# Output products put off by one step, and the first splits given to ScalarE and VectorE, in a four-stage attention and expert kernel

## The chip, the cores and the metric

One core of a Trainium2 chip runs the whole program. The metric is device time in microseconds (us), from the start to the end of one execution. Below, PE is TensorE's matmul side, PEld its weight loads, DVE is VectorE, ACT is ScalarE, POOL is GpSimd and SP is SyncE, whose queue issues the DMAs.

## What is computed

2048 tokens of width 512 go through two layers. All four parts are residual additions on `x`:

```python
x = x + L0_xattn(layernorm(x), ctx)   # 32 heads of 128, 8 key/value groups, biases
x = x + L0_ffn(layernorm(x))          # relu(x@up)**2 @ down, a latent branch, layernorm
x = x + L1_xattn(layernorm(x), ctx)   # 32 heads of 16
x = x + L1_ffn(layernorm(x))          # 8 experts, the two with the largest gate logits
```

The change is inside the first part:

```python
q = (query @ Wq + bq).reshape(B, L, NKV, G, HDIM)
k_, v_ = jnp.split(kv @ Wkv + bkv, 2, axis=-1)
attn = jax.nn.softmax(einsum('bkglm', q, k) * scale)
o = einsum('blkgd', attn, v).reshape(B, L, NHEAD * HDIM)
return o @ Wo + bo
```

## The kernel before

Every fp32 operand is split into two fp16 halves, high and low ("hi" and "lo"), and a product is three passes of fp16 matmuls (`group3`, L624): hi by hi, hi by lo, lo by hi. A product with an inner dimension of 512 is therefore 12 matmuls of 128x512. hi is written by ACT (or POOL), lo is the source less hi, written by DVE (or POOL).

The first attention runs in 32 steps `s`. A step takes one chunk of 512 tokens (8 batches of 64) for one group of four heads; the four chunks come first, then the next group. Steps 0 to 3 and 28 to 31 are written out, steps 4 to 27 are a loop of three rounds with eight steps each. Every engine has its own `b_step` with its order written by hand, and semaphores join them. On PE one step is, in this order:

- `b_scores`: 48 matmuls of 128x64 into banks 2 and 3;
- `proj(0..2)`: three of the four query projections of the **next** step (`b_proj`), into banks 0 and 1 in turn;
- `b_turn`: 16 transposes of the probabilities (L661), which need the low halves of the probabilities, `plo` on DVE (L1449, signal `s_plo`);
- `proj(3)`, `b_pv` 0 and 1 (L675, banks 6 and 7), `proj(4)` (keys), `b_pv` 2 and 3, `proj(5)` (values);
- `b_out` 0 to 3: the output products of this step, banks 4 and 5, added into `X` on DVE by `add` (L1463, signal `y_add`).

DVE's part of a step: `shift` (maximum and subtraction, L1431 and L1433, two halves), `prob` (sum, reciprocal, scaling, L1440 to L1444, two halves), `plo`, and between them the low halves of the projections (L1378; `proj(5)` is L1390), of the attention outputs (`olo`, L1378 too) and the four `add`. ACT's part: the two exponentials (L1059), `phi` (L1063), the high halves of the projections (L1024 to L1032), the copies of the turned probabilities (L1067) and of the outputs (L1038).

A projection into a bank must wait until the low half two projections back has been taken from it (`p_lo`). So `proj(2)` waits for the low half of `proj(0)`, and `proj(3)` for that of `proj(1)`.

Steps 0 and 1 have extra work: the layer norm of chunks 2 and 3 (`stats` L515 to L523, Newton steps L491 to L497, `xnorm` L535, `xlo` L542, eight transposes per tile, L554). The contexts of chunks 1 to 3 and the output weights of group 0 are split by POOL (`split_fine`, L370 to L378), the weights of group 1 by POOL as well (`group_piece`, L340 to L354), and POOL adds the output bias into `X` (`add_bo`, L399) between them. `proj(4)` of steps 0 to 2 waits for the context's low half. In the loop POOL starts on the weights of the next group when the outputs of the last one are done (`y_mm`), and on two further pieces of weights for later stages (`spare_piece`), five pieces in every four steps.

SP's queue loads in the order in which the code lists them; each load into one of the two slots of `raw` waits for the split of the piece before.

Of the kernel before, what the change touches and what calls it, by code (L numbers as in the profile page):

```python
# [67 lines left out]
def build(nc, x, ctxT, wB, wX, biasB, bo, gam, bet, lnw, be, bg, w_split, out):  # L68
    with ExitStack() as stack:
# [61 lines left out]
        staged = AW[:, 6144:10240]  # L131

# [88 lines left out]
        def _(sp):  # L221
# [20 lines left out]
            piece(4, ctxT[1], 0)  # L242
# [85 lines left out]
        def _(pool):  # L328
# [34 lines left out]
            def split_fine(conv, src, hi, lo, scale):  # L363
                n = src.shape[1]
                cuts = [slice(a, a + FINE) for a in range(0, n, FINE)]
                if scale is None:
                    pool.sem_inc(w_scaled, 1)
                else:
                    for q in cuts:
                        last = g.tensor_scalar(src[:, q], src[:, q], scale, 1.0, ALU.mult, ALU.mult)  # L370
                    last.then_inc(w_scaled, 1)
                    pool.wait_ge(w_scaled, conv + 1)
                for q in cuts:
                    last = g.tensor_scalar(hi[:, q], src[:, q], 1.0, 1.0, ALU.mult, ALU.mult)
                last.then_inc(w_hi, 1)
                pool.wait_ge(w_hi, conv + 1)
                for q in cuts:
                    last = g.tensor_tensor(lo[:, q], src[:, q], hi[:, q], ALU.subtract)  # L378
                last.then_inc(w_lo, 1)

            def landed(k):
                pool.wait_ge(raw_in[k % 2], 16 * (k // 2 - 1))

            def ctx_piece(k, c):
                landed(k)
                chunk = CT[:, c].rearrange("p s k n -> p s (k n)")
                split_fine(k, raw[:, k % 2, :], chunk[:, 0], chunk[:, 1], None)

            def group_piece(k, slot, arrivals, par, j):
# [3 lines left out]
                split(k, raw[:, slot, 0:n], hi, lo)  # L393
# [16 lines left out]
            for counted in (w_scaled, w_hi, w_lo):  # L410
                pool.sem_inc(counted, 3)
# [26 lines left out]
            for j in range(3):  # L438
                group_piece(7 + j, (7 + j) % 2, (7 + j) // 2 - 1, 1, j)
            add_bo(2)  # L440
            add_bo(3)
# [170 lines left out]
        def _(pe):  # L612
# [17 lines left out]
            def b_proj(s, c, par, j, place=None):  # L630
# [3 lines left out]
                if isinstance(s, int) and 0 < s < NC and j == 4:  # L634

                    pe.wait_ge(w_lo, s + 4)
# [28 lines left out]
            def b_pv(s, jb):  # L665
# [3 lines left out]
                if jb >= 2:  # L669
                    pe.wait_ge(o_lo, s * 4 + jb - 1)  # L670
                out_v = banks[6 + jb % 2].rearrange("p (h b l) -> p h b l", h=HG, b=2)
# [40 lines left out]
            def b_step(s, c, par, last, norm=None, split=None):  # L712
# [9 lines left out]
                b_scores(s, 1)  # L722
# [1155 lines left out]
```

## Time and profile before

| | us |
|---|---|
| median of 3 runs | 1924.45 (1923.99 to 1928.38) |
| the profiled execution | 1919.03 |
| its span, first to last instruction | 1917.2 |
| PE busy in the span | 1791.1 (93%) |
| DVE busy | 1255.0 (65%) |
| ACT busy | 894.4 (47%) |
| POOL busy | 534.5 (28%) |

Most of the runs agree closely with one another; the profiled execution is 5.4 us below the median. The trace gives start and length of each merged run of instructions on an engine, the idle time before it, and the instruction that ended this idle time. A run of 12 matmuls is listed as 2.75 us, but the next run starts 2.59 us after it: the last end is modelled and overlaps.

### The profile page before, as it was taken

The page shows a single profiled execution, that of the slowest core. Times are in us where ns is not written, and L with a number is a line of the kernel's source. Part 1 is how long each engine was busy: PE and PEld are TensorE (multiplying, and loading weights), DVE is VectorE, ACT ScalarE, POOL GpSimd, SP SyncE. Part 2 cuts the span into 40 slices and gives each one's busy share as a digit, 9 for nine tenths or more (in the row PEclk, how much of TensorE's full clock was granted, in tenths as well). Part 3 has the DMA queues.
Part 4 walks back from the last instruction along what each step waited for, and adds up shares of the span by engine and source line. Part 5 has one row for each costly group of instructions (what it writes and reads, how often), then busy time and mean ns, then how long its engine had stood idle before and what let it go on. Part 6 is the DMA issues. An engine that isn't in the chain of part 4 may idle for free. (4 is left out here: it accounts for less than half of the span.)

```text
span 1917.2 us, 36220 instructions
## 1 busy us (share of the span) xinstructions
PE 1791.1 (93%) x14128; PEld 986.1 (51%) x14128; DVE 1255.0 (65%) x2284; ACT 894.4 (47%) x1429; POOL 534.5 (28%) x403
## 2 busy tenths in 40 slices
PE   5899999999999999999999999985999999999997
PEld 2545555554555555555555444443555555555553
DVE  6785656556565556565656677767677777777763
ACT  5453434343434333343434333325666666666662
POOL 2960803407016062084000000000223222322333
PEclk9899999999999999999999999996999999999999
DMA  5220301203104012034100300030000000000000
GB/s 214 77 79 1 124 21 45 100 1 111 34 1 143 1 68 78 1 127 170 57 1 19 142 1 1 0 126 7 7 7 6 13 6 7 7 12 6 7 12 12
DMA packets 18378, 88.82 MB, mean 46 GB/s; under 512 B 2608, under 2 KB 2864, under 8 KB 10160
## 3 DMA queue, kind: packets, MB, share of 16 engines
q1 hardware_dynamic: 18224, 86.58, 12.4%
q8 instruction: 120, 1.97, 0.4%
q14 instruction: 34, 0.28, 0.0%
HBM read 65.60 MB, written 20.97 MB: 45 GB/s over the span
## 5 line engine op out<-in xcount | busy, mean ns | idle before, releaser
L624 PE MATMUL bank<-R 128*128 128x512 f16 (+1 forms) x7152 | 1301.0, 341 | 17.2 <-DVE R L1378 3.6
L624 PEld LDWEIGHTS bank<-R 128*128 128x128 f16 x7152 | 585.0, 98 | 655.9 <-issue 22.0
L1378 DVE SCALAR_TENSOR_TENSOR R<-bank,biases,R 128x512 f16<-128x512 f32 x288 | 203.2, 744 | 141.0 <-ACT R L1024 99.7
L475 POOL TENSOR_TENSOR R<-R 128x512 f32<-128x512 f32 x112 | 157.1, 1403 | 450.4 <-ACT R L1218 449.2
L1059 ACT ACTIVATE AW<-AW 128x512 f32<-128x512 f32 x64 | 40.3, 630 | 320.5 <-DVE AW L1433 320.5
L1463 DVE SCALAR_TENSOR_TENSOR X<-bank,X 128x512 f32<-128x512 f32 x128 | 88.3, 691 | 133.4 <-PE bank L624 132.5
L340 POOL TENSOR_SCALAR R<-R 128x2048 f32<-128x2048 f32 (+1 forms) x21 | 35.6, 1697 | 454.0 <-PE bank L624 450.2
L1218 ACT ACTIVATE R<-R,msk 128x512 f32<-128x512 f32 x128 | 90.3, 716 | 57.4 <-DVE R L1693 57.4
L1024 ACT ACTIVATE R<-bank,biases 128x512 f16<-128x512 f32 x128 | 87.0, 683 | 61.3 <-PE bank L624 59.9
L1390 DVE SCALAR_TENSOR_TENSOR R<-bank,R 64x512 f16<-64x512 f32 x64 | 44.0, 688 | 101.1 <-ACT R L1032 100.7
L1693 DVE SCALAR_TENSOR_TENSOR R<-bank,R 128x512 f32<-128x512 f32 x128 | 86.9, 679 | 29.0 <-PE bank L624 28.2
L1032 ACT ACTIVATE R<-bank 64x512 f16<-64x512 f32 x128 | 75.7, 592 | 56.1 <-PE bank L624 55.0
L461 POOL MEMSET R<- 128x256 f16 x1 | 0.3, 317 | 362.6 <-PE bank L624 362.6
L624 PE MATMUL bank<-CT,R 128*128 128x512 f16 x384 | 89.4, 383 | 12.7 <-DVE CT L1352 11.7
L624 PE MATMUL bank<-R,CT 128*128 128x128 f16 x1536 | 92.8, 221 | 0.0
L624 PEld LDWEIGHTS bank<-R,CT 128*128 128x128 f16 x1536 | 90.3, 99 | 1.0
L624 PE MATMUL bank<-AW,R 128*128 128x512 f16 x384 | 89.6, 384 | 1.1 <-ACT R L561 1.1
L354 POOL TENSOR_TENSOR R<-R 128x512 f16<-128x512 f32 x70 | 89.4, 1306 | 1.8
L1038 ACT ACTIVATE R<-bank,biases 128x512 f16<-128x512 f32 x128 | 80.8, 685 | 1.7 <-PE bank L675 1.7
L354 POOL TENSOR_TENSOR AW<-R,AW 128x512 f16<-128x512 f32 x64 | 77.9, 1249 | 1.3
L561 ACT ACTIVATE R<-bank 128x1024 f16<-128x1024 f16 x64 | 64.4, 1017 | 27.9 <-PE bank L554 27.9
L675 PE MATMUL bank<-AW,R 128*128 128x256 f16 x512 | 67.5, 275 | 6.4 <-DVE R L1378 5.5
(145 smaller groups left out, 2101.8 us busy)
## 6 DMA issues: line engine op xcount, KB each, us to landing
R<-in_wB SPq DMA_DIRECT2D x16, 1024.0 KB, 5.8
R<-in_wX SPq DMA_DIRECT2D x16, 1024.0 KB, 4.9
w_split<-AW SPq DMA_DIRECT2D x16, 1024.0 KB, 4.8
R<-w_split SPq DMA_DIRECT2D x12, 1024.0 KB, 7.3
R<-in_wB SPq DMA_DIRECT2D x8, 512.0 KB, 5.5
R<-in_ctxT SPq DMA_DIRECT2D x4, 1024.0 KB, 10.0
X<-in_x SPq DMA_DIRECT2D x4, 1024.0 KB, 14.1
out<-X SPq DMA_DIRECT2D x16, 256.0 KB, 2.0
```

The source lines that it names most:

```text
L354: last = g.tensor_tensor(lo[:, q], src[:, q], hi[:, q], ALU.subtract)
L475: g.tensor_tensor(acc, acc, tmp[:, e % 2, :], ALU.add).then_inc(e_acc, 1)
L561: nc.scalar.activation(dst, banks16[bank][:, 0:2 * KC * P].rearrange("p (a n) -> p a n", a=2 * KC), ACT.Copy).then_inc(n_stored, 1)
L624: last = pe.matmul(dst, a(sa), b(sb_), start=(k == 0), stop=(k == m - 1))
L675: last = pe.matmul(out_v[:, :, bb, :], V[:, b, p, :], PTb[:, b * 256:(b + 1) * 256], start=(p == 0), stop=(p == 1))
L1024: sc.activation(qT[:, 0, :, j, :], banks[j % 2].rearrange("p (b l) -> p b l", l=64), ACT.Identity, bias=bias_col(g * HG, j)).then_inc(p_hi, 1)
L1032: last = sc.activation(V[64 * half:64 * half + 64, odd:BC:2, 0, :], v[64 * odd:64 * odd + 64], ACT.Copy, scale=UN)
L1038: sc.activation(oT[:, 0, :, jb * P:(jb + 1) * P], banks[6 + jb % 2].rearrange("p (h n) -> p h n", h=HG), ACT.Identity, bias=bias_col(g, 40 ...
L1218: sc.activation(dst, tmp[:, e % 2, :], ACT.Relu, scale=msk[:, 16 + e:17 + e]).then_inc(e_rel, 1)
L1378: v.scalar_tensor_tensor(out=dst, in0=src, scalar=bias, in1=hi, op0=ALU.add, op1=ALU.subtract).then_inc(done, 1)
L1463: v.scalar_tensor_tensor(out=xt, in0=banks[4 + t % 2], scalar=UN2, in1=xt, op0=ALU.mult, op1=ALU.add).then_inc(y_add, 1)
L1693: v.scalar_tensor_tensor(out=tmp[:, e % 2, :], in0=banks[2 + e % 2], scalar=UN, in1=beb[:, e, :], op0=ALU.mult, op1=ALU.add).then_inc(e_bi ...
```

## The change

- **Output products.** For steps 0 and 1 `b_out` stays at the end of the step (`early`). The products of step 2 and later are issued in the step after: two of them behind the scores, `proj(0)`, the other two, then `proj(1)` and `proj(2)`. They use banks 6 and 7 in place of 4 and 5, which they share with `b_pv`, and the first waits for `olo(2)`, the others for `olo(3)`; `b_pv` 0 and 1 of a step wait for the last two `add` of the step before.
- **DVE.** `add_last(0)` follows `prob(0)`, `add_last(1)` follows `prob(1)`; the low half of `proj(0)` moves from behind `prob(0)` to behind `plo(1)`, and the last two additions follow it.
- **First contexts and output weights.** The split of chunk `s+1`'s context is done inside steps 0 to 2: high half on ACT behind `phi(1)` and ahead of `proj(0)`, low half on DVE behind `proj(0)` and ahead of `stats` and `proj(1)`. `proj(1)` now follows `stats`. The output weights of group 0 are split before step 0 (ACT behind the high half of the first query projection, DVE at the very end).
- **POOL.** It starts, once the projections for step 0 are done, with the key and value weights of group 1 (loaded into a place of their own, `raw_kv1`), then the query weights and the output weights, and adds the output bias chunk by chunk after the outputs of group 0 of that chunk have been added.
- **SP.** The order of the loads and their waits follow.

The diff, cut:

```diff
             x_chunk(1)
-            piece(4, ctxT[1], 0)
+            sp.dma_start(raw[:, 0, :], ctxT[1]).then_inc(raw_in[0], 16)
...
+            sp.dma_start(raw_kv1, wB[1, :, 2048:3072]).then_inc(raw_in[0], 16)
             sp.wait_ge(ctx_lo, 1)
-            piece(5, ctxT[2], 0)
-            piece(6, ctxT[3], 5)
-            for j, (a, b) in enumerate(cuts):
-                piece(7 + j, wB[1, :, a:b], 6 + j)
+            sp.dma_start(raw[:, 1, :], ctxT[2]).then_inc(raw_in[1], 16)
+            sp.wait_ge(ctx_lo, 2)
+            sp.wait_ge(ctx_hi, 2)
+            sp.dma_start(raw[:, 0, :], ctxT[3]).then_inc(raw_in[0], 16)
+            sp.wait_ge(ctx_lo, 3)
+            sp.dma_start(raw[:, 1, :], wB[1, :, 0:2048]).then_inc(raw_in[1], 16)
+            piece(9, wB[1, :, 3072:5120], 9)
...
             def add_bo(c):
+                pool.wait_ge(y_add, (c + 1) * TC)
                 for t in range(c * TC, (c + 1) * TC):
-                    pool.wait_ge(n_xn, t + 1)
...
-            pool.wait_ge(p_lo, 4)
-            pool.wait_ge(o0_in, 16)
-            split_fine(3, raw_o0, *halves(R2, 6144, 2048), WS)
-            ctx_piece(4, 1)
-            pool.wait_ge(const_in, 48)
-            add_bo(0)
-            ctx_piece(5, 2)
-            ctx_piece(6, 3)
-            add_bo(1)
...
+            pool.wait_ge(p_lo, 6)
+            group_piece(7, 0, 2, 1, 1, raw_kv1)
+            group_piece(8, 1, 2, 1, 0)
+            group_piece(9, 1, 3, 1, 2)
+            pool.wait_ge(const_in, 48)
+            for c in range(NC):
+                add_bo(c)
...
             def b_out(s, par, t):
-                pe.wait_ge(o_lo, s * 4 + t + 1)
+                pe.wait_ge(o_lo, s * 4 + (3 if t == 0 else 4))
...
-                group3(banks[4 + t % 2], [(lambda p, h=h: oT[:, p, h, t * P:(t + 1) * P],
+                group3(banks[6 + t % 2], [(lambda p, h=h: oT[:, p, h, t * P:(t + 1) * P],
...
-                for j in range(3):
-                    proj(j)
+                out(0)
+                out(1)
+                proj(0)
+                out(2)
+                out(3)
+                proj(1)
+                proj(2)
...
                 exp(0)
                 exp(1)
-                proj(0)
                 phi(0)
                 phi(1)
+                if isinstance(s, int) and s < NC - 1:
+                    act.wait_ge(raw_in[s % 2], (32, 16, 48)[s])
+                    sc.activation(CT[:, s + 1, 0].rearrange("p k n -> p (k n)"), raw[:, s % 2, :], ACT.Copy).then_inc(ctx_hi, 1)
+                proj(0)
...
                 prob(0)
-                proj(0)
+                add_last(0)
                 prob(1)
+                add_last(1)
                 plo(0)
                 plo(1)
+                proj(0)
+                add_last(2)
+                add_last(3)
+                if isinstance(s, int) and s < NC - 1:
+                    dve.wait_ge(ctx_hi, s + 2)
+                    v.tensor_tensor(CT[:, s + 1, 1].rearrange("p k n -> p (k n)"), raw[:, s % 2, :],
+                                    CT[:, s + 1, 0].rearrange("p k n -> p (k n)"), ALU.subtract).then_inc(ctx_lo, 1)
+                stats()
                 proj(1)
-                stats()
```

PE's order before, at the border of steps 2 and 3 (bank 4 and 5 with `R2,R4`: output products; bank 2 and 3 with `128x64`: scores; `R1,R2`: query projections; `ident`: the turns). These are the four output products of step 2, and then step 3:

```order
L624 MATMUL bank4<-R2,R4 128x512 x12
L624 MATMUL bank5<-R2,R4 128x512 x12
L624 MATMUL bank4<-R2,R4 128x512 x12
L624 MATMUL bank5<-R2,R4 128x512 x12
L624 MATMUL bank2<-R4 128x64 x24
L624 MATMUL bank3<-R4 128x64 x24
L624 MATMUL bank0<-R1,R2 128x512 x12
L624 MATMUL bank1<-R1,R2 128x512 x12
L624 MATMUL bank0<-R1,R2 128x512 x12
L661 MATMUL bank4<-ident,AW 128x128 x8
L661 MATMUL bank5<-ident,AW 128x128 x8
```

The same place after the change:

```order
L599 MATMUL bank2<-R4 128x64 x24
L599 MATMUL bank3<-R4 128x64 x24
L599 MATMUL bank6<-R2,R4 128x512 x12
L599 MATMUL bank7<-R2,R4 128x512 x12
L599 MATMUL bank0<-R1,R2 128x512 x12
L599 MATMUL bank6<-R2,R4 128x512 x12
L599 MATMUL bank7<-R2,R4 128x512 x12
L599 MATMUL bank1<-R1,R2 128x512 x12
L599 MATMUL bank0<-R1,R2 128x512 x12
L636 MATMUL bank4<-ident,AW 128x128 x8
L636 MATMUL bank5<-ident,AW 128x128 x8
```

The four output products now stand between the scores and the turns, where only three projections stood.

DVE's order before in step 0, from the end of `prob(0)` on (L1378: low halves of projections; L1449: `plo`; L515 to L523: `stats`):

```order
L1444 SCALAR_TENSOR_TENSOR AW<-AW,smx 128x512
L1378 SCALAR_TENSOR_TENSOR R<-bank,biases,R 128x8x64
L1440 TENSOR_REDUCE smx<-AW 128x8
L1442 RECIPROCAL smx<-smx 128x8
L1444 SCALAR_TENSOR_TENSOR AW<-AW,smx 128x512
L1449 TENSOR_TENSOR AW<-AW 128x8x64 x2
L1378 SCALAR_TENSOR_TENSOR R<-bank,biases,R 128x8x64
L515 BN_STATS cstat<-X 128x6 x4
L521 BN_AGGR cstat<-cstat 128x2 x4
L523 TENSOR_SCALAR cstat<-cstat 128x4
L1378 SCALAR_TENSOR_TENSOR R<-bank,biases,R 128x8x64 x2
```

And after (L1437, L1433, L1435, L1442 and L1371 are the old L1444, L1440, L1442, L1449 and L1378; L1508 is the low half of the context):

```order
L1437 SCALAR_TENSOR_TENSOR AW<-AW,smx 128x512
L1433 TENSOR_REDUCE smx<-AW 128x8
L1435 RECIPROCAL smx<-smx 128x8
L1437 SCALAR_TENSOR_TENSOR AW<-AW,smx 128x512
L1442 TENSOR_TENSOR AW<-AW 128x8x64 x2
L1371 SCALAR_TENSOR_TENSOR R<-bank,biases,R 128x8x64
L1508 TENSOR_TENSOR CT<-R,CT 128x2048
L490 BN_STATS cstat<-X 128x6 x4
L496 BN_AGGR cstat<-cstat 128x2 x4
L498 TENSOR_SCALAR cstat<-cstat 128x4
L1371 SCALAR_TENSOR_TENSOR R<-bank,biases,R 128x8x64 x3
```

The low half of `proj(0)` has moved behind both `plo`, and that of `proj(1)` behind the context's low half and `stats`.

## Rows read from the trace of the kernel before

**Rows 1.** The page, part 1: busy us (share of the span) xinstructions.

```profile
PE 1791.1 (93%) x14128; PEld 986.1 (51%) x14128; DVE 1255.0 (65%) x2284; ACT 894.4 (47%) x1429; POOL 534.5 (28%) x403
```

**Rows 2.** Waits of PE, 150 to 1150 us: total us, times, longest.

```profile
PE bank L661 <- DVE AW L1449: 14.9, 23, 1.0
PE bank L624 <- issue: 2.8, 2, 1.6
```

**Rows 3.** Timeline of PE: start, length, instructions, [idle before <-releaser]; turns and a loop return.

```profile
140.03 1.06 PE L661 MATMUL bank<-ident,AW 128*128 128x128 f16 x16
...
324.25 0.62 PE L661 MATMUL bank<-ident,AW 128*128 128x128 f16 x8 [0.16 <-DVE AW L1449]
325.80 0.62 PE L661 MATMUL bank<-ident,AW 128*128 128x128 f16 x8 [0.94 <-DVE AW L1449]
...
441.57 5.47 PE L624 MATMUL bank<-R 128*128 128x64 f16 x28 [1.58 <-issue]
...
1007.77 1.06 PE L661 MATMUL bank<-ident,AW 128*128 128x128 f16 x16
```

**Rows 4.** Timeline of PE, one step in which nothing waits.

```profile
387.65 1.06 PE L661 MATMUL bank<-ident,AW 128*128 128x128 f16 x16
388.55 2.75 PE L624 MATMUL bank<-R 128*128 128x512 f16 x12
391.14 1.04 PE L675 MATMUL bank<-AW,R 128*128 128x256 f16 x8
...
398.15 19.69 PE L624 MATMUL bank<-R 128*128 128x512 f16 x132
417.68 1.06 PE L661 MATMUL bank<-ident,AW 128*128 128x128 f16 x16
```

**Rows 5.** Timelines of POOL and DVE: a step with POOL at work, and one without.

```profile
315.19 1.90 POOL L340 TENSOR_SCALAR R<-R 128x2048 f32<-128x2048 f32 x1 [77.96 <-PE bank L624]
...
321.47 1.15 DVE L1444 SCALAR_TENSOR_TENSOR AW<-AW,smx 128x512 f32<-128x512 f32 x1
322.55 3.20 DVE L1449 TENSOR_TENSOR AW<-AW 128x512 f16<-128x512 f32 x2
...
1005.93 1.47 DVE L1449 TENSOR_TENSOR AW<-AW 128x512 f16<-128x512 f32 x2
```

**Rows 6.** Timelines of DVE and PE in steps 30 and 31.

```profile
999.50 0.69 DVE L1431 TENSOR_REDUCE smx<-bank 128x8 f32<-128x512 f32 x1
...
1003.10 0.69 DVE L1444 SCALAR_TENSOR_TENSOR AW<-AW,smx 128x512 f32<-128x512 f32 x1
...
1018.27 9.33 PE L624 MATMUL bank<-R 128*128 128x64 f16 x84
1028.05 2.75 PE L624 MATMUL bank<-R 128*128 128x512 f16 x12 [0.45 <-DVE X L1463]
1032.10 1.07 PE L661 MATMUL bank<-ident,AW 128*128 128x128 f16 x16 [1.31 <-DVE X L1463]
...
1020.99 1.39 DVE L1390 SCALAR_TENSOR_TENSOR R<-bank,R 64x512 f16<-64x512 f32 x2 [3.20 <-ACT R L1032]
```

**Rows 7.** Timeline of PE in step 0: the scores, and the longest wait.

```profile
47.55 11.42 PE L624 MATMUL bank<-R 128*128 128x64 f16 x84 [1.12 <-ACT R L561]
...
73.81 1.87 PE L675 MATMUL bank<-AW,R 128*128 128x256 f16 x8 [4.11 <-DVE R L1378]
```

**Rows 8.** Windows of step 0: busy us (x) of PE, PEld, DVE, ACT, POOL, then PEclk.

```profile
45.00:53.00 8.00, 6.49 (x66) 4.49 (x67) 4.82 (x9) 2.80 (x4) 7.92 (x9) 0.57 0.01 2
62.00:66.00 4.00, 4.00 (x12) 1.51 (x11) 3.26 (x10) 1.22 (x3) 3.92 (x7) 0.57 0.00 0
72.00:80.00 8.00, 6.18 (x57) 5.69 (x58) 6.56 (x8) 2.97 (x5) 8.00 (x7) 0.57 0.38 135
```

**Rows 9.** Timelines of ACT, DVE and POOL: splits of 2048 columns, and `stats`.

```profile
7.25 1.91 ACT L1015 ACTIVATE CT<-R 128x2048 f16<-128x2048 f32 x1 [1.41 <-DMA R<-in_ctxT]
...
9.19 2.29 DVE L1352 TENSOR_TENSOR CT<-R,CT 128x2048 f16<-128x2048 f32 x1 [2.10 <-ACT CT L1015]
...
28.44 2.47 DVE L515 BATCH_NORM_STATS2 cstat<-X 128x6 f32<-128x512 f32 x4
...
37.28 3.51 POOL L370 TENSOR_SCALAR R<-R 128x512 f32<-128x512 f32 x4 [24.08 <-DVE R L1378]
```

More of the change, by code:

```diff
@@ L361, in _, with group_piece @@
             FINE = 512
[L363 to L389, printed above, removed]
+            def group_piece(k, slot, arrivals, par, j, src=None):
                 alone(pool, raw_in[slot], arrivals * 16)
@@ L392, in group_piece @@
                 hi, lo = halves(R2, GW * par + off, n)
-                split(k, raw[:, slot, 0:n], hi, lo)
+                split(k, raw[:, slot, 0:n] if src is None else src, hi, lo)
             def add_bo(c):
+                pool.wait_ge(y_add, (c + 1) * TC)
                 for t in range(c * TC, (c + 1) * TC):
-                    pool.wait_ge(n_xn, t + 1)
                     g.tensor_tensor(X[:, t, :], X[:, t, :], bob, ALU.add).then_inc(bo_added, 1)
@@ L410, in _ @@
             for counted in (w_scaled, w_hi, w_lo):
[L411 to L420 removed]
+                pool.sem_inc(counted, 7)
             def spare_piece(conv, slot, arrivals, stored, row_scale=None):
@@ L670, in b_pv @@
                     pe.wait_ge(o_lo, s * 4 + jb - 1)
+                elif not (isinstance(s, int) and s == 0):
+                    pe.wait_ge(y_add, s * 4 + jb - 1)
                 out_v = banks[6 + jb % 2].rearrange("p (h b l) -> p h b l", h=HG, b=2)
@@ L679, in b_out @@
             def b_out(s, par, t):
-                pe.wait_ge(o_lo, s * 4 + t + 1)
+                pe.wait_ge(o_lo, s * 4 + (3 if t == 0 else 4))
+                if isinstance(s, int) and s == 0 and t == 0:
+                    pe.wait_ge(w0_lo, 4)
                 if t >= 2:
                     pe.wait_ge(y_add, s * 4 + t - 1)
-                group3(banks[4 + t % 2], [(lambda p, h=h: oT[:, p, h, t * P:(t + 1) * P],
+                group3(banks[6 + t % 2], [(lambda p, h=h: oT[:, p, h, t * P:(t + 1) * P],
                                            lambda p, h=h: WBo[par][:, p, h, :]) for h in range(HG)], y_mm)
@@ L722, in b_step, with out @@
                 b_scores(s, 1)
+                early = isinstance(s, int) and s < 2
+                def out(t):
+                    if not (isinstance(s, int) and s <= 2):
+                        b_out(s - 1, par if c > 0 else 1 - par, t)
                 if last:
                     for t in range(TC):
-                        b_out(s - 1, par, t)
-                    pe.wait_ge(y_add, s * 4)
+                        out(t)
                     b_turn(s, 0)
@@ L760, in b_step @@
                 proj(5)
-                for t in range(TC):
-                    if not (isinstance(s, int) and s == NG * NC - 2):
+                if early:
+                    for t in range(TC):
                         b_out(s, par, t)
-                    if t % 2 == 0:
-                        turn(t)
-                        turn(t + 1)
-                if norm is not None:
+                        if t % 2 == 0:
+                            turn(t)
+                            turn(t + 1)
                     pe.wait_ge(n_stored, norm + TC)
@@ L1136, in _ @@
             proj_hi(0, 0, 0, 2)
+            act.wait_ge(o0_in, 16)
+            w0_part(WBo[0][:, 0].rearrange("p k n -> p (k n)"), raw_o0)
             tile_hi(act, 4, 0, xnB[:, 0, :])
@@ L1392, in proj_lo, with b_step @@
                     last.then_inc(p_lo, 1)
-            def b_step(s, c, g, gn, last, norm=None):
+            def b_step(s, c, g, gn, last, norm=None, first_again=False):
                 first = None if norm is None else norm % NT
@@ L1459, in add @@
                     dve.wait_ge(y_mm, s * 4 + t + 1)
-                    if isinstance(s, int) and s < NC:
-                        dve.wait_ge(bo_added, s * TC + t + 1)
+                    if t == 0 and not isinstance(s, int) and not first_again:
+                        dve.wait_ge(bo_added, (c + 1) * TC)
                     xt = x_tile(c * TC + t)
-                    v.scalar_tensor_tensor(out=xt, in0=banks[4 + t % 2], scalar=UN2, in1=xt,
+                    v.scalar_tensor_tensor(out=xt, in0=banks[6 + t % 2], scalar=UN2, in1=xt,
                                            op0=ALU.mult, op1=ALU.add).then_inc(y_add, 1)
@@ L1495, in b_step, with add_last @@
                     return
-                    for t in range(TC):
-                        add(s, c, t)
-                    return
+                early = isinstance(s, int) and s < 2
+                def add_last(t):
+                    if not (isinstance(s, int) and s <= 2):
+                        add(s - 1, (c - 1) % NC, t)
                 shift(0)
@@ L1521, in b_step @@
                 proj(5)
-                xnorm(2)
-                for t in range(TC):
-                    if not (isinstance(s, int) and s == NG * NC - 2):
-                        add(s, c, t)
-                    if t == 0:
-                        xlo(2)
-                    if t == 1:
-                        xnorm(3)
-                        xlo(3)
+                if early:
+                    xnorm(2)
+                    add(s, c, 0)
+                    xlo(2)
+                    add(s, c, 1)
+                    xnorm(3)
+                    xlo(3)
+                    add(s, c, 2)
+                    add(s, c, 3)
             dve.wait_ge(bias_ready, 1)
```

12 lines of the change are left out of this document (6 added, 6 removed).

## The prediction

> **What bounds the kernel now.** I read the page's busy times first: PE is busy for 93% of the span and nobody else for more than 65% [rows 1], so time is saved only where PE waits or runs slowly. Next the waits of PE between 150 and 1150 us, the part with the 32 steps: the largest entry is the turn of the probabilities waiting for `plo` on DVE, 14.9 us in 23 waits, and 2.8 us are two loop returns [rows 2]. Then PE's timeline. From the turns of step 2 at 140.03 to those of step 30 at 1007.77 there are 28 steps in 867.74 us [rows 3]. One step without a wait goes from 387.65 to 417.68, which is 30.03 us [rows 4]. 28 of these are 840.84, so the 28 steps lose **26.9 us**. The loss is larger than the waits recorded [rows 2], 17.7 us, since a wait also empties the pipeline: 9.2 us over 25 waits, some 0.35 each.
>
> Why some steps wait and others don't is seen on DVE. Where POOL works in the same stretch, two `plo` take 3.20 us and one scaling L1444 1.15; without POOL 1.47 and 0.69 [rows 5, 6]. PE has only the scores and three projections between the proj(5) before them and the turns, and DVE's chain of shift, prob, plo just fits if nothing stretches it.
>
> Steps 0 to 2 are another matter: waits up to 4.11 us [rows 7], and windows with a granted clock of 0.57, a mixture of the two levels 1.2 and 2.4 GHz, each behind thin work on PE [rows 8]. Between 47.55 (scores of step 0, [rows 7]) and the turns of step 2 at 140.03 lie 92.5 us. Bare work there is 9.2 (scores and three projections of 2.59 each; the same 84 matmuls take 9.33 in [rows 6]) and two steps of 30.03 plus 1.8 for 32 transposes (16 take 0.90, [rows 4]), in sum 72.8. So these steps lose 19.7 us.
>
> **The sum, part by part.**
>
> 1. *Turn waits go.* With four output products, 4 x 2.59 = 10.4 us, between scores and turns, DVE has that much more time; the stretch by POOL is 0.46 per L1444 and 1.73 for two `plo`, in sum under 3. All 26.9 us go except the loop returns, which have nothing to do with the order: 1.58 [rows 3] and 1.2 recorded, 2.9 with refill as an estimate. **-24.0.** What is late next: point 2.
>
> 2. *A new wait, the third output product for `add_last(0)`.* It needs bank 6 back. Counting from the end of proj(5) as T: PE is ready at T + 1.40 (scores: 9.17 less 36 matmuls of 0.216) + 3 x 2.59 = T + 9.17. DVE finishes the low half of proj(5) at T + 4.1 (1020.99 + 1.39, less 1018.27, [rows 6]). From the first shift to the end of prob(0) it takes 4.2 (999.50 to 1003.79, [rows 6]), then the addition 0.69: T + 9.0, and 0.1 to hand over. The two are **level**. In step 31, where the old kernel already puts off the products, the fourth one waits 0.45 for an addition [rows 6]. Low end 0 in every step, high end 0.45 and about 0.2 of refill in every step, 18 us. I take 0.15 per step, near the low end, because the chain comes out level and not late: **+4.2**. In steps with POOL at work the 0.46 of L1444 comes on top. POOL starts after the outputs of a group, now inside the next step, and works about 45 us, so that it meets this place in one step of four, seven in all: 7 x 0.5 = **+3.5**, between 0 and 7 x 1.15.
>    The row shows that L1444 was stretched by 0.46 and not more [rows 5]. The Trainium skill, "SBUF — State Buffer", section "Who interferes with whom", has DVE and GpSimd take an exclusive lock, so that the loser waits out a whole instruction of the other. By that the price in a step is up to the 1.90 of POOL's L340 [rows 5], and point 2 would be up to 13 in place of 3.5. I stay with the row.
>
> 3. *Steps 0 to 2: the splits on the path.* These steps have no output product between scores and turns (steps 0 and 1 keep theirs at the end, step 2 has none), but `proj(2)` now waits for a low half that stands behind phi(1), the context's high half (ACT 1.91, [rows 9]) and both plo. DVE: shift 2.65 and two prob of 1.56 from T + 0.7 end at T + 6.5; phi(1) 0.6, context 1.91, high half of proj(0) 0.7, low half 0.7, with hand-overs T + 10.8. PE is ready at T + 6.6. **A wait of 4.2 us, three times, 12.6.** Then DVE does the context's low half 2.29 and the statistics 3.0 (2.47 and 0.5 of small ones, [rows 9]) before the low half of proj(1): `proj(3)` waits 2.4 in steps 0 and 1, **4.9**. The wait of b_pv 2 for `olo(0)`, 4.11 before [rows 7], shrinks to some 1 us in step 0 since POOL no longer stretches DVE's small instructions; 1.9 for both steps. POOL's query weights arrive once the context of chunk 2 is done, about 105 us, and stretch DVE in the second half of step 1 and, with the output weights, at the start of step 2: 3.4. In sum 22.8 against 19.7. Ahead of step 0 POOL's split of the output weights, which began at 37.28 [rows 9], no longer stretches DVE's `xlo` and `xnorm`: step 0 starts 1.1 earlier. ACT's share of that split, 1.91, fits into an idle time of 2.1 there, DVE's 2.3 behind the last low half, while PE runs the first scores. If that cover failed it would cost 1 to 2. Net **+2.0**.
>
> 4. *Clock in steps 0 to 2.* The 19.7 of before contain what the low level cost; the 22.8 contain none of it. The only wait of 4 us before was followed by about 6 us at the low level, PE 6.18 busy of 8 [rows 8], which is 3 us lost where PE bounds. Now there are three waits of 4.2. In steps 0 and 1 the next wait swallows most of it (1 each), in step 2 nothing does (3). Between 0 and 9; **+3.0**.
>
> 5. *Last step.* The turns no longer wait for additions (1.31, [rows 6]); the first of the last four products waits for olo(2) instead of olo(0), about 1.6. Pipeline behind them as before: **+0.8**, between -1 and 2.
>
> 6. *Nothing:* the remaining additions of the output bias run on POOL, 16 of them either way, and are waited for only at the first addition of each chunk from step 5 on, tens of us after. The weights of group 1 are needed in step 3 and done some 20 us earlier. The weights of later groups start about 15 us later in a cycle of 120 us. If any of these came late, PE would stand for the difference; the room is over 15 us in each.
>
> Sum: -24.0 + 4.2 + 3.5 + 2.0 + 3.0 + 0.8 = **-10.5 us**. Against the profiled execution, 1919.03, that is 1908.5. The median is 5.4 above this execution, and I put the forecast on it: 1924.45 - 10.5 = **1914.0 us**.
>
> **The rivals.**
>
> - *A, the third output product waits every time (slower).* Place: PE ahead of the third output product in each of 28 steps. The additions now sit in the middle of DVE's softmax chain, and each may itself wait for a product. Point 2 came out level to 0.1 us with a hand-over and, in the loop, register instructions for the wait values not counted. All but point 2 is -18.2, so it decides from 18.2 / 28 = 0.65 us per step. At the 0.94 of the old turn wait [rows 3] with refill, some 1.2 per step, it gives 33.6 - 18.2 = +15.4: 1939.9. For it: level chain, and 0.45 in step 31. Against it: in step 31 there was no proj(0) ahead of the product, now 2.59 us of cover more. 0.08.
> - *B, the clock (about no change).* Each of the three 4.2 us gaps is followed by a long stretch at 1.2 GHz, and the 2.4 us gaps too. Five stretches as in [rows 8] of 3 us each would be 15; less what the waits right behind two of them swallow, 12 in place of 3. -10.5 + 9 = -1.5: 1923. For it: every thin place before fell. Against it: the waits of step 1 before, 0.9 to 1.4 us, fell nowhere.
>   The Trainium skill, "TensorE: Matmul & The Clock Gate", section "What's actually happening", says that the half rate is the default and that activity lifts it. By that rule a change that puts idle time into three steps is paid twice; it is this rival. 0.2.
> - *C, no new wait in the steps.* DVE is early by 0.2 instead of level and POOL's stretch is harmless: without 4.2 and 3.5 the sum is -18.2: 1906. 0.2.
> - *D, the turns still wait.* The change would not do what it says, if plo moved as far back as the turns. DVE would have to lose 7 us more than in any step of the trace. With only the startup loss, +6: 1930. 0.02.
> - My forecast: 0.5.
>
> **How the numbers follow.** A measurement of this kernel can tell about 0.3%, 5.8 us, from no change. Faster by more (under 1918.7) are C, and the forecast except its end with point 2 at the high bound and the clock at 9: 0.2 + 0.43, in sum 0.63. Same takes B and part of the forecast: 0.27. Slower is A and D: 0.1. The range must leave out 0.2 at most: from 1905 (C with a cheap clock) to 1925 (B's high end); A and D and a little beyond C stay out.
>
> **What would show it.** Right: L636 (the turns) has almost no wait behind DVE after step 3; steps of 30.0 to 30.4 us without POOL; in steps 0, 1 and 2 a wait of about 4 us at the third projection and in 0 and 1 one of about 2.4 at the fourth; turns of step 2 at about 142 to 146 us. Wrong: waits for `add` (L1456) of over 0.6 us in each step; turns of step 2 later than 150 us; POOL's pieces waited for by PE.

## The result, and the profile after

| | us |
|---|---|
| median before, 8 runs | 1925.95 (1923.99 to 1928.38) |
| median after, 8 runs | 1920.48 (1919.17 to 1922.17) |
| ratio after to before | 0.9969, 95% interval 0.9959 to 0.9979 |
| profiled execution after, and its span | 1922.17, 1920.4 |
| forecast | 1914.0 (1905 to 1925) |

The change makes the kernel 5.5 to 6 us faster, where 10.5 were forecast. The sign is right and the number is inside the range, but the gain is about half of what the sum gave. A second measurement in another job, beside other runs of the kernel before, gave 1919.56 against 1927.0, ratio 0.996 (0.9943 to 0.9977), so 7 to 8 us.

The traces have to be read with care: the profiled execution of the kernel before was 6.9 us below its median, that of the changed one 1.7 above. By their spans the change even looks 3.2 us slower. The comparison therefore goes by stretches: the start up to the turns of step 2, the 28 steps to the turns of step 30, and the rest.

PE's timeline of the changed kernel in steps 0 to 2 (start us, us, engine, line, operation, [idle before <-releaser]):

```profile
11.73 5.28 PE L599 MATMUL bank<-CT,R 128*128 128x512 f16 x12 [11.73 <-DVE CT L1345]
...
58.76 5.30 PE L599 MATMUL bank<-R 128*128 128x512 f16 x12 [2.88 <-DVE R L1371]
...
98.62 4.45 PE L599 MATMUL bank<-R 128*128 128x512 f16 x12 [3.89 <-DVE R L1371]
...
104.39 2.76 PE L599 MATMUL bank<-R 128*128 128x512 f16 x12 [0.42 <-DVE R L1371]
...
115.59 1.67 PE L652 MATMUL bank<-AW,R 128*128 128x256 f16 x8 [4.98 <-DVE R L1371]
...
144.74 5.30 PE L599 MATMUL bank<-R 128*128 128x512 f16 x12 [4.06 <-DVE R L1371]
149.83 1.20 PE L636 MATMUL bank<-ident,AW 128*128 128x128 f16 x16
```

The third projection (58.76, 98.62, 144.74) waits 2.9, 3.9 and 4.1 us as forecast, and its 12 matmuls then take 5.3, 4.45 and 5.3 us in place of 2.75. The windows show why (busy us and count of PE, PEld, DVE, ACT, POOL, the granted clock, the busy share of the DMA engines and GB/s):

```profile
58.00:66.00 8.00, 7.24 (x32) 3.53 (x33) 7.19 (x13) 2.23 (x4) 0.00 (x0) 0.58 0.38 132
96.00:98.00 2.00, 0.00 (x0) 0.00 (x0) 0.31 (x2) 2.00 (x3) 0.00 (x0) 1.00 0.00 0
98.00:104.00 6.00, 5.34 (x28) 2.50 (x28) 5.96 (x12) 1.16 (x3) 0.00 (x0) 0.72 0.36 111
144.00:150.00 6.00, 5.26 (x14) 1.96 (x15) 3.54 (x3) 0.47 (x1) 0.00 (x0) 0.50 0.32 101
```

PE stands idle at the full level, and the work behind the gap runs at 1.2 GHz: 0.50 from 144 to 150, when it is busy for 5.26 of 6 us.

Then the steps. The turns that waited in [rows 3] no longer do, the loop's return has grown, and the next row of the chain has become the third output product. PE's timeline:

```profile
331.06 1.06 PE L636 MATMUL bank<-ident,AW 128*128 128x128 f16 x16
...
341.56 9.33 PE L599 MATMUL bank<-R 128*128 128x64 f16 x84
351.86 10.30 PE L599 MATMUL bank<-R 128*128 128x512 f16 x47 [0.97 <-DVE X L1456]
...
430.12 2.84 PE L599 MATMUL bank<-R,CT 128*128 128x128 f16 x48
435.98 21.34 PE L599 MATMUL bank<-R 128*128 128x64 f16 x132 [3.02 <-issue]
...
1007.99 1.06 PE L636 MATMUL bank<-ident,AW 128*128 128x128 f16 x16
1030.85 1.06 PE L636 MATMUL bank<-ident,AW 128*128 128x128 f16 x16
```

PE's waits from 150 to 1150 us (total, times, longest), beside [rows 2]:

```profile
PE bank L599 <- DVE X L1456: 6.9, 9, 1.2
PE bank L599 <- issue: 5.4, 2, 3.0
```

From the turns of step 2 to those of step 30 it is now 858.16 us, 17.3 over 28 bare steps of 30.03, where it was 26.9. Of the 28 steps 17 take 30.03 to 30.05, and step 3 takes 30.18. Eight have an addition behind POOL's work and lie 8.2 us over in sum. The two with a loop return take 34.87 and 34.05. Not all of that is idle time: behind the 3.02 us at 435.98 the 132 matmuls take 21.34 us, where they take 19.70 at the full level, and the granted clock is 0.61 from 436 to 440. Behind the other return (2.41 us idle) they take 21.14.

The wait for the addition, seen on DVE and POOL (step 8):

```profile
348.36 0.67 DVE L1433 TENSOR_REDUCE smx<-AW 128x8 f32<-128x512 f32 x1
349.06 0.20 DVE L1435 RECIPROCAL smx<-smx 128x8 f32<-128x8 f32 x1
349.30 1.81 DVE L1437 SCALAR_TENSOR_TENSOR AW<-AW,smx 128x512 f32<-128x512 f32 x1
351.04 0.68 DVE L1456 SCALAR_TENSOR_TENSOR X<-bank,X 128x512 f32<-128x512 f32 x1
```

```profile
348.68 1.89 POOL L397 TENSOR_SCALAR R<-R 128x2048 f32<-128x2048 f32 x1
350.76 2.10 POOL L406 TENSOR_SCALAR AW<-R 128x2048 f16<-128x2048 f32 x1 [0.19 <-POOL R L397]
```

L1437 normally takes 0.69. Here it starts at 349.30, while POOL's L397 runs until 350.57, and ends at 351.11, about half a microsecond after POOL's end. It waited 1.12 us, and the addition, and with it PE, came that much late.

By stretches, against the first trace of the kernel before and a second one taken later:

| | before | before, second | after |
|---|---|---|---|
| turns of step 2 | 140.03 | 140.12 | 149.83 |
| 28 steps | 867.74 | 871.00 | 858.16 |
| turns of step 30 to those of 31 | 24.33 | 24.33 | 22.86 |
| turns of step 31 to the end of the span | 885.1 | 884.9 | 889.6 |

### The profile page after: what moved, and what is told of

Its sections match the earlier page's. It is cut to its first block and busy times, and to the rows that moved or that the text cites. A ratio compares the mean times of both kernels' runs of the same rounds, so it can differ in the third digit from the quotient of the medians.

```text
span 1920.4 us, 36262 instructions
## 1 busy us (share of the span) xinstructions
PE 1795.8 (94%) x14128; PEld 988.5 (51%) x14128; DVE 1234.7 (64%) x2288; ACT 901.6 (47%) x1433; POOL 493.8 (26%) x367
## 5 line engine op out<-in xcount | busy, mean ns | idle before, releaser
L1371 DVE SCALAR_TENSOR_TENSOR R<-bank,biases,R 128x512 f16<-128x512 f32 x288 | 204.4, 745 | 264.8 <-ACT R L1012 223.9
L1051 ACT ACTIVATE AW<-AW 128x512 f16<-128x512 f32 x64 | 40.3, 630 | 87.0 <-DVE AW L1437 87.0
L360 POOL TENSOR_TENSOR R<-R 128x512 f16<-128x512 f32 x68 | 78.2, 1179 | 1.7
```

The lines of the kernel that those rows point to most:

```text
L1371: v.scalar_tensor_tensor(out=dst, in0=src, scalar=bias, in1=hi, op0=ALU.add, op1=ALU.subtract).then_inc(done, 1)
```

## The experiments

Each run changes one thing; "28 steps" is again from the turns of step 2 to those of step 30. Runs 1 to 4 shared one job, 5 to 8 another, 9 and 10 a third; the median of the kernel before was 1924.99, 1928.42 and 1927.0 there.

### 1. The kernel before, again

> The kernel before, unchanged, for a second trace. Its first profiled execution took 1919.03 us, 6.9 below the median of its runs (1925.95), while the changed kernel's took 1922.17, 1.7 above its own. Theory 1 (the clock's phase in the first 150 us differs from run to run): a second trace has its turns of step 2 some us later than 140.03, at 143 to 148, and the 28 steps to step 30 again take 867.7. Theory 2 (the difference lies in the later parts): turns of step 2 at 140 again, and the rest of the program longer by some 5 us.

Measured: 1922.17; turns of step 2 at 140.12, 28 steps 871.00, the rest as long as in the first trace. Theory 1 is wrong: the start repeats to 0.1 us. Theory 2 holds for the place, since the difference lies behind the turns of step 2, but it is 3.1 us and not 5, and all of it is in the 28 steps, which are 3.3 us longer. Single steps of 32.5 and 33.1 stand there where the first trace has 31.95 and 31.45. Behind step 30 the two traces agree. The runs of this kernel in the three jobs lie between 1919.98 and 1934.15, those of the changed one between 1915.5 and 1922.2. So the comparison of the two profiled spans is off because the kernel before scatters, and its profiled execution, at 1919.03, lay below all its other runs. That the scatter comes from how POOL's and DVE's instructions meet fits with the table but was not tested.

### 2. Only the output products put off

```diff
+                out(0)
+                out(1)
+                proj(0)
+                out(2)
+                out(3)
+                proj(1)
+                proj(2)
...
                 prob(0)
-                proj(0)
...
+                if first_steps:
+                    proj(0)
+                add_last(0)
                 prob(1)
+                add_last(1)
```

The splits of the contexts and of the output weights stay on POOL, the bias additions among them; in steps 0 to 2 everything stands as before.

> Only the output products are put off, from step 2's on, in banks 6 and 7; POOL still splits the contexts and output weights and adds the bias where it did, and in steps 0 to 2 ACT and DVE keep the old order. Theory 1 (the splits inside steps 0 to 2 cost about what the first 150 us lost, the order of the steps is the whole gain): turns of step 2 where the kernel before has them, 28 steps in about 858 as in the changed kernel, so 1914 to 1917 us, faster than the change. Theory 2 (the splits pay, since POOL no longer stretches DVE in the first steps): slower than the change, 1922 or more.

Measured: 1913.45, ratio to before 0.9933 (0.9914 to 0.9953). Turns of step 2 at 141.48, 28 steps 858.49. Theory 1, though the turns of step 2 come 1.4 us later than before, and the time is 0.5 us under what was expected. The put-off alone gains 11.5 us; the other half of the change takes about half of it back.

### 3. Only the splits and the bias additions moved

```diff
+                if first_steps:
+                    act.wait_ge(raw_in[s % 2], (32, 16, 48)[s])
+                    sc.activation(CT[:, s + 1, 0].rearrange("p k n -> p (k n)"), raw[:, s % 2, :], ACT.Copy).then_inc(ctx_hi, 1)
+                    proj(0)
...
-            split_fine(3, raw_o0, *halves(R2, 6144, 2048), WS)
-            ctx_piece(4, 1)
-            pool.wait_ge(const_in, 48)
-            add_bo(0)
-            ctx_piece(5, 2)
-            ctx_piece(6, 3)
-            add_bo(1)
...
+            pool.wait_ge(p_lo, 6)
+            group_piece(7, 0, 2, 1, 1, raw_kv1)
+            group_piece(8, 1, 2, 1, 0)
+            group_piece(9, 1, 3, 1, 2)
+            pool.wait_ge(const_in, 48)
+            for c in range(NC):
+                add_bo(c)
```

> Only the first splits go to ACT and DVE and POOL's work and the bias additions are reordered; the output products stay at the end of their step, banks 4 and 5. Theory 1: loses in steps 0 to 2 what the change loses there (three waits of 4 us at the third projection, the low clock after each), so 1928 to 1934 us. Theory 2: 1918 to 1923, faster than before.

Measured: 1933.0 (1926.61 to 1942.39), ratio 1.004 (1.0021 to 1.0058), slower than the kernel before by 8 us; the interval leaves out 1. Turns of step 2 at 152.14, 28 steps 870.05, as before. PE's waits in its first 150 us or so:

```profile
PE bank L599 <- DVE R L1363: 14.4, 5, 4.1
PE bank L650 <- DVE R L1363: 5.2, 2, 4.5
```

Theory 1. Both halves are now measured by themselves: the order of the steps is the gain, the splits are a loss of 8 to 12 us at the start (141.48 to 149.83, and 140.03 to 152.14). This run also shows what the two waits of a step have to do with each other. In step 0 the third projection runs at the full level, and the fourth waits 2.1 us, as the prediction had it:

```profile
58.58 2.76 PE L599 MATMUL bank<-R 128*128 128x512 f16 x12 [2.98 <-DVE R L1363]
...
64.34 4.41 PE L599 MATMUL bank<-R 128*128 128x512 f16 x12 [2.11 <-DVE R L1363]
```

In step 1 the third takes 5.30 us, and no wait at the fourth is recorded.

### 4. Halves of proj(0) back in their old place, in steps 0 to 2

```diff
+                first_steps = isinstance(s, int) and s < NC - 1
+                if first_steps:
+                    proj(0)
                 phi(0)
                 phi(1)
-                if isinstance(s, int) and s < NC - 1:
+                if first_steps:
...
-                proj(0)
+                else:
+                    proj(0)
...
                 prob(0)
+                first_steps = isinstance(s, int) and s < NC - 1
+                if first_steps:
+                    proj(0)
                 add_last(0)
```

> The changed kernel, with the halves of proj(0) in steps 0 to 2 taken where they were before: ACT ahead of phi(0), DVE behind prob(0). Theory 1 (that place is what makes the third projection wait 4 us and the clock fall): the waits of 2.9, 3.9 and 4.1 us at the third projection go; the one at the fourth stays or grows to some 5 us in steps 0 and 1, since the low half of proj(1) is still behind the context and stats; turns of step 2 at 141 to 144 in place of 149.8, 1914 to 1917 us. Theory 2 (the context's low half and stats hold the steps up in any case): turns of step 2 within 2 us of 149.8, time within 2 us of the change.

Measured: 1918.87 (1916.01 to 1921.37), ratio to before 0.9963 (0.9949 to 0.9977). The waits at the third projection are gone, and those at the fourth have grown to more than they had been:

```profile
65.12 4.98 PE L599 MATMUL bank<-R 128*128 128x512 f16 x12 [5.49 <-DVE R L1375]
...
105.95 5.04 PE L599 MATMUL bank<-R 128*128 128x512 f16 x12 [5.59 <-DVE R L1375]
...
117.92 1.86 PE L652 MATMUL bank<-AW,R 128*128 128x256 f16 x8 [3.46 <-DVE R L1375]
...
148.72 4.15 PE L599 MATMUL bank<-R 128*128 128x512 f16 x12 [2.74 <-DVE R L1375]
```

Turns of step 2 at 144.92, just past theory 1's 144, but 4 us of it are lost in the very next projection, still behind the context's low half (148.72): step 3's turns are at 179.26, where the changed kernel has 180.01. Theory 1's mechanism holds (the wait sits behind whatever is late in DVE's order), its time does not: 1914 to 1917 was expected, and the time is where theory 2 put it, within 2 us of the change. Moving one link of the chain moved the wait by one projection.

### 5. PE's loop return moved

```diff
+            b_step(NC, 0, 1, False, part="head")
             with pe.Fori(0, 3) as i:
                 for k in range(8):
...
-                    b_step(i * 8 + (NC + k), k % NC, 1 - k // NC, False, None, split)
+                    b_step(i * 8 + (NC + k), k % NC, 1 - k // NC, False, None, split, "tail" if k == 0 else None)
+                b_step(i * 8 + (NC + 8), 0, 1, False, None, None, "head")
```

> The changed kernel with PE's loop rotated by half a step: its return now stands between the last output product and proj(1), amid matmuls of 128x512, in place of between proj(5) (48 matmuls of 128 columns) and the scores (48 of 64 columns). The order of PE's instructions is the same. Theory 1 (the return is an instruction-side delay that is hidden only by what PE has queued ahead of it; the change put short matmuls there, so the two returns rose from about 3.4 us each with their turn waits to 4.8 and 4.0 over a step's 30.03): the issue waits of 3.0 and 2.4 us shrink to under 1 and the 28 steps take 851 to 854 in place of 858.2, so 4 to 6 us less. Theory 2 (the delay is fixed, about 1.5 to 3 us, wherever the return is): nothing above 1 us changes.

Measured: 1915.65 (1912.9 to 1917.14), ratio 0.9931 (0.9914 to 0.9948), 28 steps 852.78; the two steps with a return take 32.84 and 32.55. The same place as above, and the return itself:

```profile
430.59 2.84 PE L599 MATMUL bank<-R,CT 128*128 128x128 f16 x48
433.27 9.33 PE L599 MATMUL bank<-R 128*128 128x64 f16 x84
444.25 5.34 PE L599 MATMUL bank<-R 128*128 128x512 f16 x24 [1.65 <-DVE X L1462]
450.42 5.35 PE L599 MATMUL bank<-R 128*128 128x512 f16 x24 [0.83 <-issue]
```

Theory 1. By the traces the 28 steps are 5.4 us shorter, as forecast: 3.5 in the two steps with a return, 1.8 in the two steps behind them. The return's idle time went from 3.02 and 2.41 to 0.83 and 0.47 with the same instructions in the same order, only with long matmuls around it, and the granted clock stays at 1.00 behind it. What remains of these steps is above all an addition that is late (1.65) because DVE's own return costs it 1.82 us of idle time just before.

### 6. The additions one place earlier

```diff
+                add_last(0)
                 prob(0)
-                add_last(0)
+                add_last(1)
                 prob(1)
-                add_last(1)
```

> The changed kernel with the first addition of a late step ahead of prob(0) on DVE, and the second ahead of prob(1); nothing else. Theory 1 (in the steps in which POOL works, PE waits for the first addition behind a stretched L1437; seven to nine waits, 6.9 us recorded): the waits for L1456 fall under 1.5 us, the 28 steps take 850 to 853 in place of 858.2 (steps without POOL stay at 30.04), some 6 to 7 us less. Theory 2 (the wait then only moves to the turns or to another low half): less than 3 us.

Measured: 1911.7 (1909.51 to 1914.9), ratio 0.9914 (0.9897 to 0.9932), 28 steps 848.34. PE's waits from 150 to 1045 us:

```profile
PE bank L599 <- issue: 5.5, 2, 2.9
...
PE bank L599 <- DVE X L1456: 0.4, 1, 0.4
```

Theory 1, and even a little more than forecast: apart from the two loop returns (33.13 and 34.40) no step is more than 0.03 over 30.03, whatever POOL does. 9.8 us by the traces for swapping two pairs of lines. The expectation had 850 to 853. The late additions, with what each did to the pipeline behind it, are 8.4 of the 9.8 us. The other 1.4 is luck with the clock behind the returns:

```profile
434.95 19.70 PE L599 MATMUL bank<-R 128*128 128x64 f16 x132 [2.94 <-issue]
...
677.91 21.36 PE L599 MATMUL bank<-R 128*128 128x64 f16 x132 [2.55 <-issue]
```

Here only one of the two runs behind a return is long, in the changed kernel both were. In the six traces with the return in the changed kernel's place it is seven of twelve.

### 7. The splits ordered anew

```diff
+                if first_steps:
+                    proj(1)
                     act.wait_ge(raw_in[s % 2], (32, 16, 48)[s])
...
+                if first_steps:
+                    if norm is not None:
+                        dve.wait_ge(x_in[norm // TC], 16)
+                        for t in range(2):
+                            v.bn_stats(cbn[:, t, :], x_tile(first + t)).then_inc(n_bn, 1)
+                    proj(1)
                     dve.wait_ge(ctx_hi, s + 2)
...
+                    proj(2)
+                    if norm is not None:
+                        for t in range(2, TC):
+                            v.bn_stats(cbn[:, t, :], x_tile(first + t)).then_inc(n_bn, 1)
+                        chunk_var(dve, norm // TC)
+                    proj(3)
+                    olo(0)
+                    olo(1)
+                    if norm is not None:
+                        chunk_newton(dve, norm // TC)
+                    xnorm(0)
+                    xnorm(1)
```

The first piece is ACT's order, the others DVE's; proj(0) stands as in run 4. ACT's root of the statistics (`chunk_root`) also moves back, behind `o_part`.

> The changed kernel with steps 0 to 2 ordered anew around the same splits: halves of proj(0) and proj(1) taken ahead of the context's, half of the statistics ahead of proj(1) and half behind proj(2), the Newton steps and xnorm behind olo(1). Theory 1 (it is the place of the splits in ACT's and DVE's order that costs, not their amount): waits of 4, 5.6 and 2.4 us go, remaining ones under 1.7 us each, turns of step 2 at 132 to 137 us, 14 us less than the change: 1905 to 1909. Theory 2 (4.2 us more work per step on ACT and DVE costs wherever it stands): turns of step 2 at 140 or later, 1912 or more.

Measured: 1907.1 (1906.67 to 1907.9), ratio 0.9891 (0.9874 to 0.9907). Turns of step 2 at 133.53, 16.3 us before the changed kernel's and 6.5 before the old kernel's; 28 steps 859.66. Theory 1: the same splits on the same engines, and what costs some 10 us in one order gains 6 in another. The run also moves the halves of the projections, the statistics and their root; how much each move brings, and what the same order would bring with the splits left on POOL, was not tried. The expectation of "under 1.7 us each" missed two waits, 1.77 in step 0 and 5.32 in step 1. Ahead of the second stands the cleanest picture of what POOL does to DVE in all the runs. DVE:

```profile
100.78 0.16 DVE L472 TENSOR_TENSOR cstat<-cstat 128x4 f32<-128x4 f32 x1
100.98 4.21 DVE L510 TENSOR_SCALAR AW<-X,cstat 128x512 f32<-128x512 f32 x2
```

and POOL at the same time:

```profile
100.93 1.90 POOL L346 TENSOR_SCALAR R<-R 128x2048 f32<-128x2048 f32 x1 [48.55 <-DMA R<-in_wB]
103.02 1.90 POOL L353 TENSOR_SCALAR R<-R 128x2048 f16<-128x2048 f32 x1 [0.19 <-POOL R L346]
105.00 5.44 POOL L360 TENSOR_TENSOR R<-R 128x512 f16<-128x512 f32 x4
```

Two instructions of 0.5 us each take 4.21 us, until just after the end of POOL's second one (104.92). The first of them ends at 103.10, just after POOL's first (102.83).

### 8. Put-off, return moved, additions earlier; splits as in the kernel before

> Output products put off as in the change, first splits left to POOL as before, PE's return moved and the additions one place earlier. Theory 1: the parts add up: 858.5 for the 28 steps less some 5 and some 6, so 1901 to 1905 us. Theory 2 of either run above: 1908 or more.

Measured: 1899.68 (1895.09 to 1901.77), ratio 0.9841 (0.9821 to 0.9861), 28 steps 842.9, 2.1 over bare. Turns of step 2 at 143.31. Theory 1: the parts add up, and it is a little better than expected.

### 9. All three mends on the changed kernel

> The changed kernel with all three mends: splits of steps 0 to 2 reordered (seventh run), PE's return moved, the additions one place earlier. Theory 1 (the parts are independent): turns of step 2 at 133 to 134 as in the seventh run, 28 steps in 843 as in the eighth, so 9 to 10 us under the eighth: 1888 to 1893. Theory 2 (some of them share a gain): 1896 or more.

Measured: 1892.87 (1891.24 to 1895.4), ratio 0.9831 (0.9808 to 0.9855); turns of step 2 at 135.66, 28 steps 846.08. Theory 1, with 7 us under run 8 by the medians of the two jobs in place of 9 or 10: the turns of step 2 come some 2 us later than expected, and 3.05 us of the 28 steps are lost from step 2 to 3 (33.08), behind turns that waited 0.92 and 1.06, where the next 12 matmuls took 4.35 us in place of 2.75, as in run 7. It beats both kernels, by 34 and 27 us.

### 10. The change, again

> The changed kernel, unchanged, in the same job and beside the same runs of the kernel before. Expected: turns of step 2 at 148 to 151, 28 steps in 857 to 861, ratio to the kernel before 0.996 to 0.998. If the ratio comes out under 0.994, the first measurement understated the gain.

Measured: 1919.56 (1915.53 to 1921.9), ratio 0.996 (0.9943 to 0.9977), turns of step 2 at 150.78, 28 steps 856.76. The turns and the steps came out 0.2 below or inside what was expected, the ratio at its lower end. The first measurement stands.

## Why the prediction was half right

- **What bounds the kernel: right.** The 26.9 us of the 28 steps were there to be had: run 8 leaves 2.1 of them.
- **Point 1, turn waits go, -24.0: right.** No turn in the late steps waits in any run that puts the products off, and run 6 has 26 steps at 30.03. But its second half, that the loop returns "have nothing to do with the order", was **wrong** and is the largest single miss: 2.9 us were left for the two of them, and the two steps came out 8.9 us over bare ones, +6.0. Ahead of the return there stood 48 matmuls of 128x512, 10 us of queued work; the put-off left 48 matmuls of 128 columns, 2.7 us. The idle time at the two returns rose from 2.8 us to 5.4, and the work behind it, which ran at the full level before, took 3.1 us more (21.34 and 21.14 for 19.70). The sum had the clock in steps 0 to 2 only. Run 5 shows both by moving the return.
- **Point 2, a new wait for `add_last(0)`, +4.2 and +3.5: the sum came out (8.5 for 7.7) by luck, the parts are wrong.** PE and DVE did come out level there: steps without POOL lose 0.01 us, not 0.15. With POOL it is 8.2 us in eight steps, not 3.5. The price of one stretch was taken from a single row, 0.46 of [rows 5], against the rule of the Trainium skill ("SBUF — State Buffer", "Who interferes with whom"), which the text had set aside. By the rule the loser waits out the other's whole instruction. The rows above decide for it: 1.12 us lost on L1437 until POOL's L397 was done, and 4.21 for two instructions of 0.5 behind two of 1.90. The 0.46 was one draw from between 0 and 1.9.
- **Point 3, steps 0 to 2, +2.0, and 4, clock, +3.0: mechanism right, together +9.8 instead of +5.0.** The three waits (2.9, 3.9, 4.1 for 4.2) and their place were right. The waits of 2.4 at the fourth projection almost vanished (none in step 0, 0.4 in step 1), since the third ran at the low level meanwhile; in run 3, where it once ran at the full level, the fourth waited 2.1. What was mis-sized is the stretch by POOL in step 1: three of the four Newton steps took 1.0 to 1.1 for 0.16 and b_pv 2 waited 4.98, where 1 and part of 3.4 had been allotted; and the clock, which fell behind each of the three gaps and again in step 1 (a window of 0.57 at 116 to 120). The Trainium skill's rule on the clock ("TensorE: Matmul & The Clock Gate", "What's actually happening"), by which this idle time is paid twice, agrees with these rows, though not every gap is paid twice: in run 3 the 12 matmuls behind 2.98 us of idle time took 2.76. Rival B was right about the place. Its price of 12 us was not reached: behind the three gaps it is 6.8, in step 1 another 1.8. The 1.1 us gained ahead of step 0 can't be seen in the sum: the scores start at 47.54, as before, because the very first matmuls took 5.28 us for 4.07. Between runs 2 and 3, whose first matmuls took the same, it is 0.8 (48.15 and 47.34).
- **Point 5, last step, +0.8:** the turns come 1.47 earlier, the first of the last four products waits 1.53 for olo(2), and the next stage starts 0.4 late, counted from the turns of step 30. Right, within its bounds.
- **Behind it**, from the turns of step 30 to the end, all nine traces that put the products off take 911.8 to 913.8 us, the three that don't 909.3 to 910.2. Point 5 had 0.8 of these 3.0; the other 2.2 was in no term. In the two traces compared here 0.4 arises in the last step, 0.9 at the passage to the second attention and 1.7 in the last matmuls of all. Before and after, the same instructions:

```profile
1315.26 4.26 PE L624 MATMUL bank<-AW,R 128*128 128x512 f16 x12 [1.12 <-ACT R L561]
1889.40 20.88 PE L624 MATMUL bank<-R 128*128 128x512 f16 x96
```

```profile
1315.90 5.21 PE L599 MATMUL bank<-AW,R 128*128 128x512 f16 x12 [1.12 <-ACT R L536]
1890.82 22.57 PE L599 MATMUL bank<-R 128*128 128x512 f16 x96
```

  They run longer at a lower granted clock (0.66 from 1890 to 1895, where the kernel before has 1.00). Why it fell there is open; in seven of the nine traces the last 96 take 20.88, and the time is lost earlier.

So by the traces: +9.8 - 9.6 + 3.0 = +3.2. The sum had -10.5, a miss of 13.7 (the parts are rounded): 6.0 for the returns, 0.8 for point 2, 4.8 for points 3 and 4, 2.2 behind. 1908.5 + 13.7 is the 1922.2 that the profiled execution took. The forecast missed by only half of that, because it put the gain "on the median", 5.4 us above the execution that the sum was made against. So it is luck that 1920.48 lies near the forecast: the sum was far off for the execution that it was made against, and this execution was an unusually fast one. What the kernel before loses in its usual executions and not in that one lies, in the one other trace, in the same 28 steps; that the put-off takes it away fits with the medians and is not shown by itself. The step that failed is above all point 1's clause on the loop returns, then the size of points 3 and 4.

## What to carry to other kernels

Work put between a producer chain and its consumer removes the wait, but look at what it moves elsewhere: at what stands in the queue ahead of a loop return, and at the instructions that now stand in the middle of the chain. A split or a statistic on a busy engine can cost ten microseconds or gain six (runs 3 and 7), depending on which low half stands behind it; follow each buffer back to the next write into it. And when VectorE and GpSimd share a stretch, price a meeting by GpSimd's longest instruction, not by the mean.

## What the runs showed of the hardware

- A meeting of POOL and DVE costs the DVE instruction the rest of POOL's, several times its own length (0.69 became 1.81, two of 0.50 became 4.21). Not every DVE instruction pays: in step 8 the reduction L1433, at 348.36, and the reciprocal behind it ran beside POOL's L397 and took their usual 0.67 and 0.20. It goes the other way too: POOL's first piece of 1024 columns, 1.05 us otherwise, took 2.88 while DVE's split of 2048 columns ran from 46.01 for 2.28 us:

```profile
46.31 2.88 POOL L346 TENSOR_SCALAR AW<-AW 128x1024 f32<-128x1024 f32 x1 [32.69 <-DVE R L1371]
```

- How long PE stands idle at a loop return depends on what is queued around it: 2.41 to 3.09 us with 48 matmuls of 128 columns just ahead (twelve returns in six traces), 0.83 and 0.47 amid matmuls of 512 columns (run 5), and none is recorded in runs 8 and 9, which have the same place. With 48 matmuls of 512 columns ahead, as in the kernel before, it is 1.05 to 1.76, recorded only behind the first 43 or 44 of the next step's scores. Since the count ahead is 48 both times, it isn't the number alone; that it is the time of the queued work fits and was not separated from what stands behind the return.
- Such an idle time can be paid a second time: behind seven of those twelve returns the next 132 matmuls took 20.98 to 21.36 us, behind the other five 19.70.
- The kernels with the products at the end of their step scatter most: the kernel before over 4.4 us in 8 runs, but 11 to 14 in sets of 11 to 23, and run 3 over 15.8 in 12. Those with the products put off scatter over 1.2 to 6.7 us in sets of 5 to 12. The late additions are not what decides among these: run 7 has them and scatters least, run 8 has none and scatters most. The cause is open.
